# Eight sets of expert weights instead of four: buffers laid over the residual and both token operands, loaded eight experts ahead at first and four ahead in the loop

## The reference

```python
x = L0_attn_x
x = x + selective_scan(layernorm(x), ...)        # 16 states, a scan over the tokens
x = x + hadamard_ffn(layernorm(x), ...)          # 512 -> 2 x 2048 -> 512
x = x + mixer(layernorm(x), W_in, conv_w, ...)   # 512 -> 2 x 1024 -> 512
x = x + moe(layernorm(x), gate_w, wg, wu, wd)    # 64 experts, top 8
```

```python
probs = softmax(x @ gate_w.T);  w, sel = top_k(probs, 8);  w = w / sum(w)
# every expert takes its first 128 tokens (CAP = 128); the rest are dropped
inp = the 128 rows of each of the 64 experts
h = silu(inp @ wg[e]) * (inp @ wu[e])            # 512 -> 192
out = h @ wd[e]                                  # 192 -> 512
y[token] += out * w
```

## Time and profile before

| what | value |
|---|---|
| median of 3 runs | 1786.7 us (1778.75, 1786.7, 1788.29) |
| the profiled execution | 1787.74 us, of which its span is 1785.9 us |
| mean granted clock of PE | 0.937 |
| PE busy | 1524.0 us, 85% |
| DVE, ACT, POOL busy | 1060.5, 588.9, 793.9 us |
| moved by DMA | 380.35 MB, mean 213 GB/s |

### The profile page before, as it was taken

How to read it: one execution, slowest core, us unless ns; L and a number is a source line. 1 busy time by engine, 2 the same in 40 slices (tenths; PEclk the granted TensorE clock), 3 DMA queues, 4 the chain that set the end, 5 groups by cost and what they waited for, 6 DMA issues and landing times. The chain is left out here.

```text
span 1785.9 us, 19377 instructions
## 1 busy us (share of the span) xinstructions
PE 1524.0 (85%) x5792; PEld 1038.8 (58%) x5792; DVE 1060.5 (59%) x1588; ACT 588.9 (33%) x1031; POOL 793.9 (44%) x491
## 2 busy tenths in 40 slices
PE   6989966888867899988999899999992798889992
PEld 2444423566645677777787787778771454445551
DVE  3787688776589887788898855552453122222220
ACT  4434533353534354544333322121210222222220
POOL 3256753355653354644455424663276222222222
PEclk8999988999977999999999999999995899999997
DMA  6677553368773577667565557997640699999997
GB/s 197 168 209 210 143 183 125 114 198 278 241 222 97 169 221 212 195 197 259 162 184 172 167 180 259 356 336 235 205 122 25 202 321 305 283 289 312 318 320 130
DMA packets 193536, 380.35 MB, mean 213 GB/s; under 512 B 20994, under 2 KB 95106, under 8 KB 192944
## 3 DMA queue, kind: packets, MB, share of 16 engines
q1 hardware_dynamic: 173424, 339.44, 60.9%
q0 software_dynamic: 20032, 39.92, 9.3%
HBM read 301.65 MB, written 124.35 MB: 239 GB/s over the span
## 5 line engine op out<-in xcount | busy, mean ns | idle before, releaser
L1427 POOL TENSOR_TENSOR y<-y,hc 128x2048 f32<-128x2048 f32 x64 | 292.9, 4577 | 286.1 <-DVE hc L1268 286.1
L575 PE MATMUL bank<-tokT,ring 128*128 128x512 f32 x768 | 309.5, 403 | 15.4 <-DVE xall L1125 7.1
L1250 DVE TENSOR_TENSOR_SCAN bx<-bank,state,bx 128x512 f32<-128x512 f32 x256 | 312.6, 1266 | 0.8
L577 PE MATMUL bank<-tokT,ring 128*128 128x512 f32 x768 | 304.3, 396 | 0.0
L576 PE MATMUL bank<-tokT,ring 128*128 128x512 f32 x768 | 303.6, 395 | 0.0
L925 ACT ACTIVATE bank<-dl,an 128x512 f32<-128x512 f32 x256 | 171.0, 684 | 321.9 <-DVE bx L1250 321.9
L1433 POOL TENSOR_TENSOR act<-th,act 128x512 fp32r<-128x512 f32 x96 | 126.1, 1314 | 276.1 <-ACT act L849 275.7
L575 PEld LDWEIGHTS bank<-tokT,ring 128*128 128x128 f32 x768 | 147.1, 192 | 53.0 <-issue 19.7
L803 PE MATMUL bank<-wgu,xeT 128*128 128x384 f32 x512 | 177.0, 489 | 0.0
L587 PE MATMUL bank<-ring,act 128*128 128x512 f32 x360 | 149.1, 414 | 29.8 <-DVE th L1114 27.1
L577 PEld LDWEIGHTS bank<-tokT,ring 128*128 128x128 f32 x768 | 146.7, 191 | 32.4
(11 more groups left out here) (145 smaller groups left out, 2037.4 us busy)
## 6 DMA issues: line engine op xcount, KB each, us to landing
ring<-w_all SPq DMA_DIRECT2D x288, 512.0 KB
wgu<-wgu_in SPq DMA_DIRECT2D x64, 768.0 KB
wde<-wd_in SPq DMA_DIRECT2D x64, 384.0 KB
slots<-empty_in SPq DMA_DIRECT2D x16, 1154.0 KB, 8.6
xe<-slots SPq DMA_DIRECT2D x64, 288.5 KB
w_all<-staged_u SPq DMA_DIRECT2D x64, 256.0 KB, 2.8
w_all<-fst SPq DMA_DIRECT2D x48, 256.0 KB, 3.5
w_all<-staged_d SPq DMA_DIRECT2D x32, 256.0 KB, 3.2
```

The source lines that it names most:

```text
L575: nc.tensor.matmul(b[:, :], w[:, k, 0, :], x[:, 0, k, :], start=(k == 0), stop=False)
L577: last = nc.tensor.matmul(b[:, :], w[:, k, 1, :], x[:, 0, k, :], start=False, stop=(k == KT - 1))
L1250: nc.vector.tensor_tensor_scan(bx[:, k, :], dA[k % 2][:, :], bx[:, k, :], state[:, k, n:n + 1], ALU.mult, ALU.add).then_inc(S_sc, 1)
L1427: nc.gpsimd.tensor_tensor(y[c % 2][:, :, :], y[c % 2][:, :, :], hc[:, :, :], ALU.add).then_inc(S_ya, 1)
```

## The change

There are eight sets of weights (DEEP = 8), each in buffers of its own, `wgu0` to `wgu7` and `wde0` to `wde7`. Sets 0 to 3 lie where the four sets lay. Sets 5 and 6 lie in the first 20 KB of `xall`, set 4 in `tokT0` and set 7 in `tokT1`, so they can be loaded only when those are no longer needed. Set 4 is loaded at TURN+14; set 5 at TAIL-6, when the normalised rows of tile 9 are made and three chunks of the residual are stored; set 6 at TAIL-1, when those of tile 11 are made; set 7 at TAIL+2. In the loop SP issues the rows of expert e and then, after the wait for the down product of e-4, both weight transfers of expert e+4. For the last four experts it issues rows alone. One semaphore for each set counts both weight transfers, so the gate and up product waits for `wde` too. The loop bodies hold eight experts in place of four; rows keep their four buffers.

```diff
+DEEP = 8
+            wgu, wde = [None] * DEEP, [None] * DEEP
+            def expert_buffers(slots):
+                with ExitStack() as ctx:
+                    for i in slots:
+                        wgu[i] = sb(ctx, f"wgu{i}", [P, KT, 2 * FE])
+                        wde[i] = sb(ctx, f"wde{i}", [FH, 2, D])
+            expert_buffers((5, 6))
             xall = sb(A, "xall", [P, NCH, TT, D])
...
+            expert_buffers((4,))
             tokT = [sb(A, "tokT0", [P, 2, KT, CH], f32r)]
...
+            expert_buffers((7,))
             tokT.append(sb(A, "tokT1", [P, 2, KT, CH], f32r))
-            with ExitStack() as expert_weights:
-                wgu = sb(expert_weights, "wgu", [P, SLOTS, KT, 2 * FE])
-                wde = sb(expert_weights, "wde", [FH, SLOTS, 2, D])
+            expert_buffers((0, 1, 2, 3))
...
                     def load_weights(e, i):
-                        sp.dma_start(wgu[:, i, :, :], a["wgu"]...).then_inc(S_gu[i], 16)
-                        if not isinstance(e, int):
-                            sp.wait_ge(S_y, e - SLOTS + 1)
-                        sp.dma_start(wde[:, i, :, :], a["wd"]...).then_inc(S_dn[i], 16)
+                        if not isinstance(e, int) or e >= DEEP:
+                            sp.wait_ge(S_y, e - DEEP + 1)
+                        sp.dma_start(wgu[i][:, :, :], a["wgu"]...).then_inc(S_ew[i], 16)
+                        sp.dma_start(wde[i][:, :, :], a["wd"]...).then_inc(S_ew[i], 16)
...
                         for i in range(SLOTS):
                             if pos == DRAIN + 16 + 8 * i:
                                 load_weights(i, i)
+                        if pos == TURN + 14:
+                            load_weights(4, 4)
+                        if pos == TAIL - 6:
+                            sp.wait_ge(n4.xn, 2 * TT + 2)
+                            sp.wait_ge(S_x3, 16 * 3)
+                            load_weights(5, 5)
+                        if pos == TAIL - 1:
+                            sp.wait_ge(n4.xn, 3 * TT)
+                            load_weights(6, 6)
+                        if pos == TAIL + 2:
+                            load_weights(7, 7)
...
-                    with sp.Fori(1, E // SLOTS) as q:
-                        for i in range(SLOTS):
-                            e = SLOTS * q + i
-                            sp.wait_ge(S_ws, e - SLOTS + 1)
-                            sp.wait_ge(S_gm, e - SLOTS + 1)
-                            load_rows(e, i)
-                            load_weights(e, i)
+                    def refill_expert(e, i, last=False):
+                        sp.wait_ge(S_ws, e - SLOTS + 1)
+                        sp.wait_ge(S_gm, e - SLOTS + 1)
+                        load_rows(e, i % SLOTS)
+                        if not last:
+                            load_weights(e + SLOTS, (i + SLOTS) % DEEP)
+                    for i in range(SLOTS, DEEP):
+                        refill_expert(i, i)
+                    with sp.Fori(1, E // DEEP - 1) as q:
+                        for i in range(DEEP):
+                            refill_expert(DEEP * q + i, i)
+                    for i in range(DEEP):
+                        refill_expert(E - DEEP + i, i, last=(i >= SLOTS))
...
                     def gate_up(q, i):
-                        pe.wait_ge(S_gu[i], 16 * (q + 1))
+                        pe.wait_ge(S_ew[i], 32 * (q + 1))
...
                     def down(q, i):
-                        pe.wait_ge(S_dn[i], 16 * (q + 1))
```

More of the change, by code:

```diff
@@ L220, in build @@
             S_xe = [sem(f"rows_in{i}") for i in range(SLOTS)]
-            S_gu = [sem(f"gate_up_in{i}") for i in range(SLOTS)]
-            S_dn = [sem(f"down_in{i}") for i in range(SLOTS)]
+            S_ew = [sem(f"expert_in{i}") for i in range(DEEP)]
             S_xt = sem("rows_transposed"); S_xc = sem("rows_copied"); S_gm = sem("gate_up_mm"); S_et = sem("e_tanh")
@@ L328, in previous @@
                 def previous(q, i):
-                    return (q, i - 1) if i else (q - 1, SLOTS - 1)
+                    return (q, i - 1) if i else (q - 1, DEEP - 1)
                 def following(q, i):
-                    return (q, i + 1) if i + 1 < SLOTS else (q + 1, 0)
+                    return (q, i + 1) if i + 1 < DEEP else (q + 1, 0)
                 def steps(eng, f):
-                    for i in range(SLOTS):
+                    for i in range(DEEP):
                         f(0, i, first=(i == 0))
-                    with eng.Fori(1, E // SLOTS - 1) as q:
-                        for i in range(SLOTS):
+                    with eng.Fori(1, E // DEEP - 1) as q:
+                        for i in range(DEEP):
                             f(q, i)
[L341 to L349, removed]
+                    for i in range(DEEP):
+                        f(E // DEEP - 1, i, last=(i == DEEP - 1))
                 @block.sync
@@ L482, in load_weights @@
                     def load_weights(e, i):
-                        sp.dma_start(wgu[:, i, :, :], a["wgu"].rearrange("e p k f -> (e p) k f")[ds(e * P, P), :, :]).then_inc(S_gu[i], 16)
-                        if not isinstance(e, int):
-                            sp.wait_ge(S_y, e - SLOTS + 1)
-                        sp.dma_start(wde[:, i, :, :], a["wd"].rearrange("e p s h -> (e p) s h")[ds(e * FH, FH), :, :]).then_inc(S_dn[i], 16)
+                        if not isinstance(e, int) or e >= DEEP:
+                            sp.wait_ge(S_y, e - DEEP + 1)
+                        sp.dma_start(wgu[i][:, :, :], a["wgu"].rearrange("e p k f -> (e p) k f")[ds(e * P, P), :, :]).then_inc(S_ew[i], 16)
+                        sp.dma_start(wde[i][:, :, :], a["wd"].rearrange("e p s h -> (e p) s h")[ds(e * FH, FH), :, :]).then_inc(S_ew[i], 16)
                     for pos in range(LAST):
@@ L789, in rows_T @@
                     def rows_T(q, i):
[L790 to L791 removed]
+                        e = DEEP * q + i
+                        pe.wait_ge(S_xe[i % SLOTS], 16 * (DEEP // SLOTS * q + i // SLOTS + 1))
                         wait(pe, S_xc, e - 1)
                         for k in range(KT):
[L794 removed]
+                            last = nc.tensor.transpose(CX[i % 2][:, k * P:(k + 1) * P], xe[:, i % SLOTS, k * P:(k + 1) * P], ident[:, :])
                         last.then_inc(S_xt, 1)
                     def gate_up(q, i):
[L798 to L799 removed]
+                        e = DEEP * q + i
+                        pe.wait_ge(S_ew[i], 32 * (q + 1))
                         pe.wait_ge(S_xc, e + 1)
@@ L802, in gate_up @@
                         for k in range(KT):
-                            last = nc.tensor.matmul(CG[i % 2][:, 0:2 * FE], xeT[:, i % 2, k, :], wgu[:, i, k, :],
+                            last = nc.tensor.matmul(CG[i % 2][:, 0:2 * FE], xeT[:, i % 2, k, :], wgu[i][:, k, :],
                                                     start=(k == 0), stop=(k == KT - 1))
@@ L820, in down @@
                         for s in range(2):
-                            last = nc.tensor.matmul(CO[i % 2][:, :], hT[:, i % 2, s, :], wde[:, i, s, :], start=(s == 0), stop=(s == 1))
+                            last = nc.tensor.matmul(CO[i % 2][:, :], hT[:, i % 2, s, :], wde[i][:, s, :], start=(s == 0), stop=(s == 1))
                         last.then_inc(S_y, 1)
@@ L834, in _ @@
                     steps(pe, step)
-                    h_T(E // SLOTS - 1, SLOTS - 1)
-                    down(E // SLOTS - 1, SLOTS - 1)
+                    h_T(E // DEEP - 1, DEEP - 1)
+                    down(E // DEEP - 1, DEEP - 1)
                 @block.scalar
@@ L1064, in down @@
                     def down(q, i):
-                        e = SLOTS * q + i
+                        e = DEEP * q + i
                         act.wait_ge(S_y, e + 1)
                         act.wait_ge(S_ws, e + 1)
-                        if not (isinstance(q, int) and q == 0):
-                            act.wait_ge(S_add[i % 2], 16 * (2 * q + i // 2 - 1))
-                        nc.scalar.activation(ye[:, i, :], CO[i % 2][:, :], ACT.Copy, scale=wsc[:, i:i + 1]).then_inc(S_ys, 1)
+                        wait(act, S_add[i % 2], 16 * (DEEP // 2 * q + i // 2 - 1))
+                        nc.scalar.activation(ye[:, i % SLOTS, :], CO[i % 2][:, :], ACT.Copy, scale=wsc[:, i % SLOTS:i % SLOTS + 1]).then_inc(S_ys, 1)
                     def step(q, i, first=False, last=False):
@@ L1389, in gated @@
                     def gated(q, i):
-                        e = SLOTS * q + i
-                        dve.wait_ge(S_xe[i], 16 * (q + 1))
+                        e = DEEP * q + i
+                        dve.wait_ge(S_xe[i % SLOTS], 16 * (DEEP // SLOTS * q + i // SLOTS + 1))
                         wait(dve, S_ys, e - SLOTS + 1)
[L1393 to L1397, removed]
+                        wait(dve, S_add[i % 2], 16 * (DEEP // 2 * q + i // 2 - 1))
```

(2 more changed lines are left out.)

10 lines of the change are left out of this document (5 added, 5 removed).

## The result

The changed kernel is slower: 1801.63 us in the median of four runs (1791.07 to 1807.02) against 1787.15 of the kernel before, ratio 1.0099 with a 95% interval of 1.0051 to 1.0147. Run again (e1) it gave 1794.37 against 1779.47, 1.008 (1.0035 to 1.0124). That is 14.5 and 14.9 us; the forecast was 0.9 us, with 1796 us as the upper end. The times given are medians of all runs, but a ratio leaves out runs more than 1.5% above the fastest of their kernel, which matters for e7 (4 of 12 left out; the medians of all runs stand at 0.9925, not 0.9893), e17 and e18 (4 of 21 of the kernel before left out; 1.0067 and 0.9916).

The account below looks back on a forecast made before the run. PE was taken to wait for rows in SP's full DMA queue from expert 11 on. Start +2.4 us and end -1.5 gave +0.9 on 1787.74, 1788.6; predicted median 1787.6 us, range 1776 to 1796.

Parts of the forecast that it names:

- The drain: Stretch before the expert loop: the added prefetch and its waits cost 0, and the loop starts no later.
- The start: Start of the expert loop: wgu is issued later, so later rows land 2.4 us later; bounds 0 and 5.3 us.
- The end: Last four experts: no weights behind their rows, so PE runs at its own pace; gain 1.5 us, bounds 0 and 2.9.
- The pace: Steady expert loop: same three transfers per round, PE waits for rows, so pace unchanged at 5.69 us an expert: 0.
- rival 2: Expert loop: reading weights four experts away lowers the engines' rate under about 300 GB/s; 12 us more, 1799; chance 0.14.
- Where the prefetch went: Expert loop: the 4.72 MB loaded ahead disappear only from the last four steps, when the queue is empty anyway.
- 1: Expert loop: bytes alone count, four sets fewer end it 14.7 us earlier, 1772 (half: 1779); chance 0.19 in full or half.
- 3: Tail before the loop: prefetch delays the last ring load, PE waits up to 3.6 us more, 1791; within the forecast's 0.67.

Follow-up runs that it names:

- e7: Kernel before (four sets), with the loop's rows issued by ScalarE through a queue of their own: 1766.1 us, ratio 0.9893.
- e17: Changed kernel with wde issued ahead of wgu, both still behind the wait, then the rows: 1793.01 us, ratio 1.0064.
- e18: e8 (eight sets, rows on ScalarE's queue) with wde issued ahead of wgu: 1766.01 us, ratio 0.9936 against the kernel before.
- e11: Changed kernel with wgu ahead of the wait for experts 8 to 11 only: 1792.27 us, ratio 1.0066 against the kernel before.
- e4: Changed kernel reading weights from expert 8 on from the place of the expert four before (wrong output, same bytes): 1797.05 us, ratio 1.0107.
- e2: Changed kernel with the old order, wgu ahead of the wait for the down product, eight sets kept: 1781.49 us, ratio 1.0026.
- e3: Kernel before (four sets, no prefetch) with the wait for the down product moved ahead of wgu: 1798.15 us, ratio 1.0116.
- e9: e8 (eight sets, rows on ScalarE's queue) with the old order, wgu ahead of the wait: 1762.78 us, ratio 0.9904.
- e10: e7 (four sets, rows on ScalarE's queue) with the wait for the down product ahead of wgu: 1781.91 us, ratio 1.0004.
- e14: e10 (four sets, rows on ScalarE's queue, both weights behind the wait) with wde ahead of wgu: 1755.19 us, ratio 0.984.
- e5: Kernel before, with rows and wgu issued after the gate and up product, wde of the expert before after its wait: 1789.5 us, ratio 1.0048.
- e6: Changed kernel (eight sets), with rows and wgu issued ahead of the wait, wde of e+3 after it: 1786.28 us, ratio 1.0027.
- e8: Changed kernel (eight sets), with rows from expert 4 on issued by ScalarE through their own queue: 1780.96 us, ratio 1.0011.
- e13: Kernel before, with wgu issued one step later, behind the next expert's rows (order wde, rows, wgu; one queue): 1784.4 us, ratio 1.0026.

## Why the prediction was wrong

**The drain.** Right: no wait of SP, no later start of the loop.

**The start.** The mechanism held (first wait for rows at expert 7 or, in the chain, 8; nothing issued for a step). The term was 2.4 us, measured 3.9 up to expert 12. By then four or five steps at the slower pace are in it, some 0.28 us each, which is about the difference. e11, which takes back this term alone, reached expert 12 2.3 us sooner, in one profile.

**The end.** Right: 1.5 us forecast, 1.7 measured between experts 60 and 63 (means of 16.6 and 14.9 us), PE at its own pace from expert 60.

**The pace: the step that failed.** I wrote "An expert's traffic is the same three transfers in the same round", and from that "Pace unchanged, 5.69 us: 0". The cyclic round g, d, r is indeed the same, and the bytes, the addresses' distance (e4) and the fullness of the engines don't matter or don't change. But the round is issued in bunches, and the change moved the cut: the bunch that had ended with `wgu` now ends with the rows. With it went the rate, from between 302 and 319 GB/s to between 289 and 298, and 12.9 us on 46 steps (11, give or take 7, with the one-edit kernels). The single edits e2 and e3 show that the order of `wgu` and the wait does this; that it acts through the end of the bunch fits e9, e10 and e14 and is less sure in one queue (e5, e6). I kept 5 us for the pace, as chance to either side, and rival 2 named an outcome like this one (a mean under 300 GB/s, 12 us, 1799) for another cause, the addresses, which e4 rules out. That rival got 0.14.

**Where the prefetch went.** The argument that four sets fewer shorten only the last four steps is borne out by the profile after (steps at 4.96 us from 60 on). But I gave the queue's order as the reason, and there e8 and e9 speak against me: with rows free to pass, eight sets (e9 0.9904, e18 0.9936) are no better than four (e7 0.9893, e14 0.984), although four sets of traffic are missing from the loop. The chains tell what held them: from 1460 to 1680 us, in e8, e9 and e18, and in e7 too, they consist almost wholly of the additions to `acc`, each of which POOL issues when the last into that table has landed. In e9 one for two experts takes 9.4 to 10.5 us, 5.25 us a step in all. Weights that are there four experts early don't shorten that. The lead of four experts never paid.

**Rivals.** 1 fell. 3 fell. 2 was right in size and wrong in cause.

**What stays open.** Why full engines move less when the last transfer of a bunch is a small one. The loss lies in the packets of the weights. By the start and duration of each packet from 1460 to 1680 us, a 6 KB packet of `wgu` took 286, 265 and 287 ns in the mean in the three profiles of the kernel before and 296, 308 and 298 in those of the changed one. A 4 KB packet of `wde` took 206, 196 and 198 against 215, 225 and 222. The packets of the rows took no longer (132, 123, 129 against 124, 128, 122), nor did the 2 KB packets of the additions (176 to 177 in all six). Whether the engines work on one transfer together doesn't explain it. At a moment at which a `wgu` packet is moved, 9.0 to 10.6 are in flight in the kernel before and 8.0 to 8.6 in the changed one (11.3 and 11.6 in e7 and e14, 7.9 in e10). But there are 11.4 in e13 at 310 GB/s, 8.0 in e6 at 307 and 9.2 in e18 at 324. Also open is whether the moment of issue against POOL's additions plays a part: no run moved that alone. Nor was it tried why, with rows on ScalarE, the additions that set the pace take longer with eight sets (9.3 to 10.9 us in e9 and e18) than in e7 (8.8 to 9.7).

## What to carry to other kernels

When a DMA-bound loop's transfers are regrouped, take the delivered GB/s as unknown even if bytes, sizes and cyclic order stay: here one moved wait alone was worth 1%, with the engines' busy share at 1.05 throughout. Try a bunch that ends with its largest transfer, and try the rows or other small urgent transfers on another engine's queue: here that gave 1.1%, and 1.6% together with the better order, where four more buffers gave nothing. Before crediting a deeper prefetch, ask at which step of the loop its bytes are missing; here only behind the last fetch that anything waited for. And one profile of each kernel would have shown next to nothing of this loss: compare times of many runs, and make the single edits.

## What the runs showed of the hardware

- Sixteen DMA engines at a busy share of 1.05 or 1.06 moved between 289 and 336 GB/s of the same traffic (e1, e7), by order and queue and, within one kernel, by execution (302 to 319).
- Two hardware queues (weights from SP, rows from ScalarE) beside the software one moved 324 to 336 GB/s (e7, e9, e14, e18) where one had moved 302 to 319, if the weights' bunch ended with `wgu`; otherwise 305 and 307 (e8, e10).
- One kernel's executions differ by more than an edit's effect: 1763.59 to 1799.04 us for the kernel before in one set of 21 runs, and 302 to 319 GB/s in its loop. With four runs of each the sign was clear; for the division into terms even three profiles of each were few.
